# A gated block-linear layer with LoRA: bias as data in the accumulators, a third plain row pair, and a last product in two column halves

## The reference: what is computed

```
xn    = (x - mean) / sqrt(var + 1e-5)                  # per row
s     = xn @ (W * blockmask).T + bias                  # W 1024 x 1024, 32 x 32 blocks switched on or off by a mask
base  = xn @ W_org.T                                   # W_org 1024 x 1024
coef  = softmax(mean over the rows of a batch (xn) @ Wq.T @ keys.T / sqrt(128))   # 8 experts, one set per batch
delta = xn @ (sum over experts of coef * lora_down * lora_up)
out   = x + s * silu(base + delta)
```

## Time and profile before

| what | value |
|---|---|
| median of the runs | 451.86 us |
| profiled execution | 449.17 us |
| its span | 447.4 us |
| TensorE (PE) busy | 431.2 us, 96% of the span |
| PE weight loads busy | 342.7 us, 77% |
| VectorE busy | 345.6 us, 77% |
| ScalarE busy | 225.2 us, 50% |
| GpSimd busy | 86.6 us, 19% |
| HBM traffic | 226 GB/s over the span |

### The profile page before, as it was taken

How to read it: one execution, slowest core, us unless ns; L and a number is a source line. 1 busy time by engine, 2 the same in 40 slices (tenths; PEclk the granted TensorE clock), 3 DMA queues, 4 the chain that set the end, 5 groups by cost and what they waited for, 6 DMA issues and landing times.

```text
span 447.4 us, 5868 instructions
## 1 busy us (share of the span) xinstructions
PE 431.2 (96%) x1882; PEld 342.7 (77%) x1882; DVE 345.6 (77%) x488; ACT 225.2 (50%) x398; POOL 86.6 (19%) x86
## 2 busy tenths in 40 slices
PE   6699989899999999999999999999999999999995
PEld 6247767687777777878888888888888888888883
DVE  3899899879888888746566988877577699777735
ACT  3897887857534434333233854353522466453421
POOL 5104312200010121040015010024410220032510
PEclk9899999999999999999999999999999999999999
DMA  8996973554867588699631526788996312356583
GB/s 295 422 412 189 324 264 117 191 187 187 281 223 250 212 304 286 214 391 377 197 101 58 164 72 207 246 291 292 409 405 221 115 46 67 114 172 219 173 274 115
DMA packets 40870, 101.59 MB, mean 227 GB/s; under 512 B 4612, under 2 KB 4612, under 8 KB 40072
## 3 DMA queue, kind: packets, MB, share of 16 engines
q1 hardware_dynamic: 40840, 101.23, 65.2%
HBM read 71.85 MB, written 29.36 MB: 226 GB/s over the span
## 4 chain that ended last, share of the span: by engine, by line
PE 86%; DMA 5%; ACT 3%; DVE 2%; issue 2%; SPq 1%; POOL 0%; ACTq 0%; DVEq 0%
PE psA L819 27%; PE psA L821 27%; PE psA L820 27%; DMA bias_raw<-in_bias_dram 3%; PE psA L905 2%; PE psA L921 2%; DMA xn_dram<-xq 1%; DMA xq<-in_x_t_dram 1%; PE psM L864 1%; ACT b_hi L1031 1%; DVE b_lo L1161 0%; ACT x_nat_sb L972 0%; ACT masks L998 0%; PE psM L855 0%; PE psM L871 0%
## 5 line engine op out<-in xcount | busy, mean ns | idle before, releaser
L819 PE MATMUL psA<-b_hi,a_hi 128*128 128x512 f32 x440 | 174.2, 396 | 3.3 <-DVE b_lo L1161 1.4
L821 PE MATMUL psA<-b_hi,a_lo 128*128 128x512 f32 x440 | 171.5, 390 | 0.0
L820 PE MATMUL psA<-b_lo,a_hi 128*128 128x512 f32 x440 | 171.2, 389 | 0.0
L819 PEld LDWEIGHTS psA<-b_hi,a_hi 128*128 128x128 f32 x440 | 82.6, 188 | 23.3 <-issue 3.4
L821 PEld LDWEIGHTS psA<-b_hi,a_lo 128*128 128x128 f32 x440 | 82.6, 188 | 17.6
L820 PEld LDWEIGHTS psA<-b_lo,a_hi 128*128 128x128 f32 x440 | 82.7, 188 | 16.4
L1031 ACT ACTIVATE b_hi<-b_raw 128x512 fp32r<-128x512 f32 (+2 forms) x66 | 45.8, 717 | 53.6 <-DVE b_raw L1174 30.7
L1161 DVE TENSOR_TENSOR b_lo<-b_raw,b_hi 128x512 fp32r<-128x512 f32 (+2 forms) x66 | 52.0, 811 | 8.5 <-ACT b_hi L1031 8.0
L1060 ACT ACTIVATE snaps<-psA 128x512 f32<-128x512 f32 x42 | 25.0, 595 | 57.2 <-PE psA L821 46.2
L1225 DVE TENSOR_TENSOR cst<-psA,snaps 128x512 f32<-128x512 f32 x42 | 28.7, 686 | 28.2 <-ACT snaps L1060 18.8
L1161 DVE TENSOR_TENSOR a_lo<-s_raw,a_hi 128x512 fp32r<-128x512 f32 x56 | 40.9, 744 | 8.5 <-ACT a_hi L1021 8.5
(11 more groups left out here) (116 smaller groups left out, 500.0 us busy)
## 6 DMA issues: line engine op xcount, KB each, us to landing
xn_dram<-xq SPq DMA_DIRECT2D x16, 512.0 KB, 3.9
s_dram<-cst SPq DMA_DIRECT2D x32, 256.0 KB, 3.3
worg_sb<-in_w_org_dram SPq DMA_DIRECT2D x32, 256.0 KB, 3.5
xq<-xn_dram SPq DMA_DIRECT2D x16, 512.0 KB, 5.2
s_in<-s_dram SPq DMA_DIRECT2D x32, 256.0 KB, 4.1
xres<-in_x_nat_dram SPq DMA_DIRECT2D x32, 256.0 KB, 4.6
out_dram<-cst SPq DMA_DIRECT2D x32, 256.0 KB, 3.9
x_nat_sb<-in_x_nat_dram SPq DMA_DIRECT2D x14, 512.0 KB, 4.2
```

The source lines that it names most:

```text
L819: nc.tensor.matmul(ps, l_hi, r_hi, start=first, stop=False, skip_group_check=True)
L820: nc.tensor.matmul(ps, l_hi, r_lo, start=False, stop=False, skip_group_check=True)
L821: return nc.tensor.matmul(ps, l_lo, r_hi, start=False, stop=over, skip_group_check=True)
```

## The change

Five things are done at once.

- Bias. It is loaded as 128 equal rows (512 KB in place of 16 KB). The matmuls of line 921 and the small steps for their operands are gone. The blocks of plain pairs get the bias in their copy (QC, now an addition). For the groups with 7 products ACT or DVE write the bias, or the difference of its halves, into the bank ahead of products 1 and 5 (step PB, 10 times), and these products accumulate onto it. BD is now that difference; it waits until the copies of the plain pairs have used the old values.
- `WFIRST = 3`: pair 2 is plain as well. Tiles 4 and 5 are turned by TX; their LT, X, XR, BA, BP, BC and N steps are gone.
- The products (15, 5) and the last, (15, 3), are made in two halves of 256 columns; the second halves of their bank lies in psM. The steps after the last product run for each half (TQ, TF, TM, TR, TS).
- The loads at the start stand in another order, and so do the first steps of all engines.
- The five lists of `ORDER` are new.

The core of the diff:

```diff
-WFIRST = 2
+WFIRST = 3
...
-    LX0 LX1 LM0 LW0.0 LW0.1 LM1 LI LW1.0 LX3 LX2 LW1.1 LM2 LW2.0 LM3 LW3.0 LY LX4 LX5 RS1 RS0 ST2 RS2 LX7 ST3 LT6
+    LX0 LM0 LW0.0 LW0.1 LX1 LM1 LM2 LW1.0 LX2 LW1.1 LX3 LW2.0 LM3 LI LW3.0 LY LX4 RS0 LX5 RS1 RS2 ST2 RS3 LT7 LX6
...
+    LAST = len(prods) - 1
+    HALF = H // 2
+    HALVES = (index[(GROUPS - 1, 5)], LAST)
...
+        def last_bank(h):
+
+            return tail(psM[:, len(misc_use) % MISC, :] if h else bank_of(LAST), h)
...
+        def bias_into(eng, u, y):
+
+            key = ("XY"[y], u)
+            k = acc_use[key]
+            if k >= ACC:
+                wait_acc_free(eng, acc_order[k - ACC])
+            eng.wait_ge(bias_loaded, 16)
+            if y:
+                eng.wait_ge(dve_step, 1)
+            return acc_bank(key), bias_sb[:, y, :]
...
+                    biased = WFIRST <= u < 8 and i in (1, 5)
+                    bank = take_acc(acc_key(n)) if first and not biased else bank_of(n)
+                    if biased:
+                        wait_bias(pe, u, int(i == 5))
...
+                    if n in HALVES:
+                        slot = m % ARING
+                        if first:
+                            wait_misc_free(pe, misc_order[-MISC])
+                        for h in range(2):
+                            for c in range(4):
+                                cols = slice(c * P, (c + 1) * P)
+                                ins = triple(last_bank(h), a_hi[:, slot, cols], a_lo[:, slot, cols],
+                                             tail(b_hi[:, to, c, :], h), tail(b_lo[:, to, c, :], h), c == 0 and first, c == 3)
+                            if h == 0 and n == LAST:
+                                ins.then_inc(pe_half, 1)
+                        ins.then_inc(pe_P, 1)
+                        continue
...
-                    if biased:
-                        pe.wait_ge(act_ones, 1)
-                        pe.wait_ge(dve_bias, 1)
-                        v, rows = biased
-                        ins = nc.tensor.matmul(bank, ones_r[0:rows, :], bias_rows[0:rows, v, :], start=False, stop=True,
-                                               skip_group_check=True)
...
-                if kind == "BI":
-                    act.wait_ge(pool_sign, 1)
-                    act.wait_ge(bias_loaded, 16)
-                    nc.scalar.activation(ones_r[:, :], ones[0:4, :], ACT.Copy, scale=row_sign[:, 1:2]).then_inc(act_ones, 1)
-                    mine(nc.scalar.activation(bias_hi[:, :, :], bias_raw[:, :, :], ACT.Copy))
-                    nc.scalar.activation(bias_raw[:, :, :], bias_raw[:, :, :], ACT.Copy, scale=row_sum[:, 1:2])\
-                        .then_inc(act_bias, 1)
+                if kind == "PB":
+                    bank, values = bias_into(act, *st[1:])
+                    nc.scalar.activation(bank, values, ACT.Copy).then_inc(act_bias, 1)
...
-                        nc.vector.tensor_copy(cst_of(n), bank_of(n)).then_inc(dve_post, 1)
+                        dve.wait_ge(bias_loaded, 16)
+                        nc.vector.tensor_tensor(cst_of(n), bank_of(n), bias_sb[:, i[1], :], ALU.add).then_inc(dve_post, 1)
```

More of the change, by code:

```diff
@@ L118 @@
[L118 to L122, removed]
@@ new lines @@
+    BP11 BP12 P30 P31 BP13 P32 P33 P34 P35 BP14 BP15 P36 P37 P38 P39 P40 P41 P42 P43 P44 P45 P46 P47 P48 P49 P50
+    P51 G0 P52 P53 P54 P55 G1 P56 P57 P58 E0.0.2 E0.1.2 E0.2.2 E0.3.2 E0.0.0 E0.0.1 E0.1.0 E0.1.1 E0.2.0 E0.2.1
+    E0.3.0 E0.3.1 E0.0.3 E0.1.3 E0.2.3 E0.3.3 P59 P60 P61 P62 P63 P64 P65 P66 P67 P68 P69 P70 P71 P72 P73 P74 P75
+    P76 P77 P78 P79 P80 P81 P82 P83 P84 P85 P86 E1.0.2 E1.1.2 E1.2.2 E1.3.2 E1.0.0 E1.0.1 E1.1.0 E1.1.1 E1.2.0
+    E1.2.1 E1.3.0 E1.3.1 E1.0.3 E1.1.3 E1.2.3 E1.3.3 P87 P88 P89 P90 P91 P92 P93 P94 P95 P96 P97 P98 P99 P100 P101
@@ L511, in wait_rows, with wait_split @@
                 eng.wait_ge(dve_N, n_num[(t,)] + 1)
+        def wait_split(eng, t):
+            for kh in range(2):
+                eng.wait_ge(pe_P, index[(0, (t, 0, kh))] + 1)
+                wait_lo(eng, ("A", op_num[("a", 0, t, kh)]))
         def wait_x(eng, u, half, kh=None):
@@ L687, in free_xq @@
                 if before == 0:
-                    for kh in range(2):
-                        sp.wait_ge(pe_P, index[(0, (half, 0, kh))] + 1)
-                        wait_lo(sp, ("A", op_num[("a", 0, half, kh)]))
+                    wait_split(sp, half)
                 if before < 8:
@@ L812, in _ @@
                           .then_inc(stored[k % CST], 16)
+                elif kind == "TS":
+                    h = st[1]
+                    half, nh = block_done(prods[LAST])
+                    sp.wait_ge(dve_half, tr_num[(h,)] + 1)
+                    sp.dma_start(out[2 * (prods[LAST][0] - 8) + half][:, nh * H + h * HALF:nh * H + (h + 1) * HALF],
+                                 tail(cst_of(LAST), h)).then_inc(half_stored, 16)
+            sp.wait_ge(half_stored, 32)
             for k in range(CST):
-                sp.wait_ge(stored[k], 16 * len([n for n in block_seq if block_seq[n] % CST == k]))
+                sp.wait_ge(stored[k], 16 * len([n for n in block_seq if block_seq[n] % CST == k and n != LAST]))
         @block.tensor
@@ L1068, in _ @@
                         .then_inc(act_post, 1)
+                elif kind == "TF":
+                    h = st[1]
+                    act.wait_ge(dve_half_sum, tq_num[(h,)] + 1)
+                    nc.scalar.activation(tail(cst_of(LAST), h), tail(cst_of(LAST), h), ACT.Silu).then_inc(act_half, 1)
                 elif kind == "QF":
@@ L1088, in _ @@
                 if kind == "BD":
-                    dve.wait_ge(act_bias, 1)
-                    nc.vector.scalar_tensor_tensor(bias_rows[:, :, :], bias_hi[:, :, :].bitcast(F32), row_sign[:, 0:1],
-                                                   bias_raw[:, :, :], ALU.mult, ALU.add).then_inc(dve_bias, 1)
+                    dve.wait_ge(bias_loaded, 16)
+                    for n in block_seq:
+                        if prods[n][0] < WFIRST and prods[n][1][1]:
+                            wait_block(dve, n)
+                    nc.vector.tensor_tensor(bias_sb[:, 1, :], bias_sb[:, 1, :], bias_sb[:, 0, :], ALU.subtract)\
+                        .then_inc(dve_step, 1)
+                elif kind == "PB":
+                    bank, values = bias_into(dve, *st[1:])
+                    nc.vector.tensor_copy(bank, values).then_inc(dve_bias, 1)
                 elif kind == "SN":
```

209 lines of the change are left out of this document (122 added, 87 removed).

## The result

The kernel after takes 440.1 us (median of 4 runs, 438.64 to 441.44), the kernel before 452.1 us on the same chip: a ratio of 0.974, 95% interval 0.970 to 0.978. The profiled execution took 438.64 us with a span of 436.9, 10.5 under the 447.4 of before. The forecast was 443.5 us in a range of 439.5 to 449.0, with a sum of -8.3 us: the direction and the range held. The kernel gained 2.2 us more in the profile than the sum said, and 3.7 more by the medians (12.0).

A forecast was written before the change was run, and what follows sets the result against it. PE, 86% of the chain that ended last, was taken as the bound. Terms -10.8 + 2.7 + 1.9 + 0.6 - 0.5 - 3.2 + 0.5 + 1.5 - 1.0 = -8.3 us from 451.86 gave 443.5, range 439.5 to 449.

The forecast's parts named there:

- 18 bias matmuls: Bias matmuls outside the opening: removing them saves PE 0.60 us each, -10.8 us (-7.7 to -11.5).
- transposes less BP: Pair 2 made plain: 16 more transposes for tiles 4 and 5, +2.3, less two BP pairs, -0.4: +1.9 us.
- halves: Last products: 48 matmuls of 256 columns for 24 of 512, at 0.125 us between starts: +0.6 us (0 to 5.4).
- opening: Start up to P4: earlier P1 and fewer bias matmuls against a possible lower clock: -0.5 us (-1.5 to +1.5).
- three waits gone: PE's waits of 1.4, 1.0 and 0.8 us between 59 and 89 us, for weight splits, would go: -3.2 us.
- BD and bank Y of group 3: Behind the last plain copy, the bias difference and bank fill might come late: 0.5 us left for it.
- first E product: PE would wait for the `down` chain's split, store and loads, taking 12 to 17 us: +1.5 us (0 to 4.5).
- end: After the last matmul's start: half-wide steps and a smaller store, -1.0 us (-0.3 to -1.6).
- rival 3: Gaps belong to a product's end; a bias matmul is worth only 0.226 us: sum -1.6, 450.3 us; chance 0.04.
- Rival 1: Waits come back; E wait and opening take their upper ends, +3.0 and +2.0: 448.5 us; chance 0.12.
- Rival 2: Half-width matmuls are held by their weight loads at nearly the old distance, +4.8: 448.3 us; chance 0.08.
- Rival 4: `down` chain becomes the bound: last split at 188, PE at 194 waits 9 to 12 us: 453.5 to 454; chance 0.06.

The follow-up runs named there:

- run 1: Kernel before with its 20 bias matmuls left out, nothing else changed: ratio to before 0.979, span 439.6 us.
- run 3: Kernel after with a 4-row matmul of 512 columns added behind 20 products: 452.76 us, ratio to before 1.003.
- run 2: Kernel before with 18 of its 20 bias matmuls replaced by a matmul on the product's operands: ratio to before 0.988 with 128 rows, 0.999 with 64.
- run 4: Kernel before with the bias part of the change alone (bank fills, bias added in copies), otherwise in the order of before: 454.1 us, ratio to before 1.007.
- run 5: The kernel of run 4 with the weight split that PE waited for moved ahead of the scaling of tile 5: 451.96 us, ratio to before 1.001.
- run 8: Kernel after with the first of the four loads that the first E product needs put fourth in the queue: 447.2 us, ratio to before 0.987.
- Run 10: Kernel after with the original weight needed first at the second E block loaded first: 438.7 us (0.971 to before); with a reordered opening too, 438.1 us (0.970).
- run 7: Kernel after with the opening reordered (tile 1 transposed, copied and scaled earlier): 440.5 us, ratio to before 0.975.
- run 9: Kernel after with its last two products whole again, one copy chain and one store: 441.9 us, ratio to before 0.980.

## Why the prediction was right, and by its steps

The mechanism held: bias matmuls dear by their few rows, and a kernel bound by PE whose helpers keep up. That the sum came within 2.2 us of the profile's 10.5 is in part luck: two reserves for waits that did not come (2.0 us) stood against one wait that nobody looked for (1.1 us), and the other terms erred by 1.3 us in the same direction.

| term | forecast | found | from |
|---|---|---|---|
| 18 bias matmuls | -10.8 | -11.1 | what the other rows leave of P4 to the last matmul; 0.60 and 0.66 each by runs 1 and 3, so 10.8 to 11.8 |
| product of pair 2 | +2.7 | +2.7 | 12 x 0.226 |
| transposes less BP | +1.9 | +1.4 | 0.89, twice 0.45, less two BP pairs at the forecast's 0.2 |
| halves | +0.6 | +0.3 | 24 x (2 x 0.120 - 0.226) |
| opening | -0.5 | -0.6 | P4 at 33.88 for 34.49, within the scatter |
| three waits gone | -3.2 | -3.2 | list of waits |
| BD and bank Y of group 3 | +0.5 | 0 | no wait between P4 and 326 us |
| first E product | +1.5 | 0 | E at 190.4 follows without a gap |
| second E block | none | +1.1 | wait at 328 us |
| end | -1.0 | -1.05 | 4.86 for 5.91 |

By the medians 12.0 us were gained and not 10.5, since the profiled execution of before lay 3.0 us under its median and that of after 1.5.

**The bias matmul.** Runs 1 and 3 show 0.60 to 0.66 us each, and run 2 that the cause is its few rows. Its choice against the rule of 0.226 (rival 3) was decided by reading the gap on both sides of the instruction in the earlier trace rows.

**The waits.** That they would go was the least supported step, and the one that carries the result: the same saving gave nothing before K in the order of before (run 1), and less than nothing with the fills and additions (runs 4 and 5). The reason given, that DVE and ACT get less to do in turn, is half borne out: from 34.5 to 90 us ACT is busy 38.3 us for 44.3, DVE 50.4 for 51.1, while PE starts 261 matmuls for 228. It was priced at the 3.2 us of waits that could be seen. The worth of the third pair and the new lists together is larger: in run 1, without them, the waits grew by 2.9 us and cost 1.4 us of clock besides.

**The first E product.** The step failed in size: 12 to 17 us for the chain, which took 8.7. In the kernel before it took 17.1 us, so the range described the old lists. In the new ones each part is shorter: the store goes 1.4 us after the start of the split instead of 3.4, the load that E needs is first and no longer third and goes 2.9 us behind the store instead of 5.7, and it lands in 4.4 instead of 8.0, the fastest of the eight. The forecast took the landing times of all eight loads, though only this one has to be there. That the chain was near was right: the slack is 1.2 us, and run 8 turned three places in a queue into some 6 us.

**What was not seen.** The second block of E was not looked at, because before had no wait there. PE arrives earlier, and four loads wait for blocks that come when PE has finished them, in a stretch (260 to 330 us) where the transfer share is 0.92 and was 0.79 before. Run 10 shows that the wait hangs on the order of these loads and of the steps behind them; what share the fuller transfer engines have in it is open.

**The rivals.** Rival 1 held in kind (a wait came back) and not in size. Rival 2 fell: 0.120 between starts. Rival 3 fell by run 2. Rival 4 fell: D0 came at 105.1 as it said, but the last split at 180.5 and not 188. The chain took 75.4 us for 83.1, so it kept no fixed pace. PE came even sooner than rival 4 had it, at 190.4 and not 194.

## What to carry to other kernels

Price a small instruction by the starts of its neighbours, not by its length: here the short matmul lasts 0.50, and costs 0.64. When PE-bound work is removed, mark an instruction that stands behind the same work in both kernels (here K) and ask engine by engine whether the helpers can follow; if they can't, taking work from them may pay even when it gives PE more (here the third pair and the new lists did so together). And for every chain that does not start from PE, write down its slack at the point where PE needs it, here 5 us before and 1.2 after: with such a slack, one load moved back by three places costs some 6 us.

## What the runs showed of the hardware

- A matmul with 2, 4 or 64 rows between 128-row matmuls of 512 columns moves its neighbours apart by 0.4 us more than a 128-row one; with 128 rows there is no gap.
- Matmuls of 256 columns with their own weight loads start 0.120 us apart, about half of the 0.226 of 512 columns, though a weight load is shown as lasting 0.19.
- A wait of PE can cost more than its length. After waits of 2.8, 2.9 and 4.0 us (runs 1, 7, 8) the granted clock fell about 1.2 us after PE resumed, and the matmuls ran at the lower of its two levels (a granted clock of 0.50, 1.2 instead of 2.4 GHz) for some 3 us, seven steps of 0.43, 1.4 us; the waits of 4.8, 3.2 and 3.7 us of runs 4 and 5 were followed by it as well. After waits of 1.0 to 1.45 us it stayed at full. Between, it went both ways: 2.4 us was followed by full clock with 128 rows and by half clock with 64 (run 2), 1.9 us by full clock in run 9 and by half in run 8. What decides was not tried.
